# Edge counting of a GPS layer: one-hot tiles made eight at once, two moves on GpSimd's queue, edge slots in two halves

## The reference, cut to what matters

```
xn = layernorm(x)
# graph convolution: 20,625 edges (src, dst), sorted by dst, loops included
deg  = segment_sum(1, dst);  norm = deg[src]^-1/2 * deg[dst]^-1/2
gnn  = segment_sum((xn @ W)[src] * norm, dst) + b
# attention, 12 heads, 266 features
k1 = ratio * (exp(k' - diag_k - max over ALL of k') + 1e-4)     # one maximum for the whole of k'
q1 = ratio * (exp(q' - diag_q - max over features) + 1e-4)
mix = (q1 @ (k1^T v)) / (q1 @ sum k1) @ W_proj + b_proj
x1 = x + gnn + mix
out = x1 + experts(layernorm(x1))      # shared expert plus three of 15 routed ones
```

## Time and profile before

| what | value |
|---|---|
| median of three runs | 1266.8 us (1265.02 to 1268.58) |
| the profiled execution's own time | 1266.61 us |
| its span, first to last instruction | 1264.9 us |
| PE busy, PE weight load | 1146.0 us (91%), 1006.5 us (80%) |
| DVE, ACT, POOL busy | 788.2, 660.2, 499.5 us |
| mean granted TensorE clock | 0.961 |

### The profile page before, as it was taken

The page is one execution under the profiler, slowest core; times in us unless marked ns, Lnnn a source line. Parts: engine busy times, 40 slices in busy tenths (PEclk is TensorE's granted clock), DMA queues, the critical chain, the costliest instruction groups (busy, mean ns, idle before and its releaser), DMA issues.

```text
span 1264.9 us, 20941 instructions
## 1 busy us (share of the span) xinstructions
PE 1146.0 (91%) x6438; PEld 1006.5 (80%) x6439; DVE 788.2 (62%) x1478; ACT 660.2 (52%) x1042; POOL 499.5 (39%) x351
## 2 busy tenths in 40 slices
PE   2999946999549899999999999999999999999985
PEld 1999946887435557888889998888999888899974
DVE  7832613256399584662586597465596698655983
ACT  4122617236210303443687668566677796676863
POOL 1078877888630050026232243121343272323421
PEclk9899977999879899999999999999999999999998
DMA  9030000550110012212678666647657887386943
GB/s 311 1 84 2 2 2 2 138 172 6 15 75 2 1 58 92 88 25 55 219 263 321 225 210 241 201 149 280 214 205 282 306 321 229 134 307 215 347 164 96
DMA packets 62948, 191.72 MB, mean 152 GB/s; under 512 B 14172, under 2 KB 15239, under 8 KB 62902
## 3 DMA queue, kind: packets, MB, share of 16 engines
q1 hardware_dynamic: 50134, 172.52, 37.2%
q0 software_dynamic: 11728, 18.27, 8.2%
q10 hardware_dynamic: 1040, 0.33, 0.1%
HBM read 178.74 MB, written 15.09 MB: 153 GB/s over the span
## 4 chain that ended last, share of the span: by engine, by line
PE 58%; POOL 17%; DVE 10%; issue 7%; DMA 3%; ACT 2%; ACTq 0%; SPq 0%; DVEq 0%; POOLq 0%
PE banks L1910 23%; PE banks L1894 22%; POOL edge_dram L721 17%; PE banks L1832 3%; DVE ohd L966 3%; PE banks L1878 2%; DVE ohs L965 2%; PE banks L1882 2%; PE banks L1804 2%; DMA out<-ysb,sidx 2%; PE banks L1871 1%; PE banks L1652 1%; DVE w2lo L525 1%; DMA xs<-in_x 1%; DMA xn_dram<-xn 1%
## 5 line engine op out<-in xcount | busy, mean ns | idle before, releaser
L721 POOL DMA_INDIRECT edge_dram<-epair,eslot x165 | 216.1, 1310 | 111.1 <-DVE eslot L936 61.4
L800 POOL DMA_INDIRECT out<-ysb,sidx x27 | 118.8, 4399 | 237.1 <-issue 205.8
L512 ACT ACTIVATE w2hi<-w2raw 128x1536 fp32r<-128x1536 f32 x96 | 139.2, 1483 | 90.4 <-DMA w2raw<-in_L_ffn_fc_w 78.9
L525 DVE TENSOR_TENSOR w2lo<-w2raw,w2hi 128x1536 fp32r<-128x1536 f32 x96 | 164.3, 1752 | 22.9 <-ACT w2hi L512 20.7
L1910 PE MATMUL banks<-w2hi,hthi 128*128 128x384 f32 x624 | 161.4, 339 | 0.0
L1910 PE MATMUL banks<-w2lo,hthi 128*128 128x384 f32 x624 | 159.1, 335 | 0.0
L1910 PE MATMUL banks<-w2hi,htlo 128*128 128x384 f32 x624 | 158.9, 335 | 0.0
L512 ACT ACTIVATE w1hi<-w1raw 128x1536 fp32r<-128x1536 f32 x96 | 137.2, 1495 | 27.3 <-DMA w1raw<-in_L_ffn_fc_w 24.7
L525 DVE TENSOR_TENSOR w1lo<-w1raw,w1hi 128x1536 fp32r<-128x1536 f32 x80 | 147.7, 1910 | 0.2 <-DVE xs L1128 0.2
L1894 PE MATMUL banks<-w1hi,xthi 128*128 128x512 f32 x486 | 139.7, 396 | 3.0 <-POOL w1lo L525 3.0
L1894 PE MATMUL banks<-w1lo,xthi 128*128 128x512 f32 x486 | 136.8, 390 | 0.0
(11 more groups left out here) (338 smaller groups left out, 1956.3 us busy)
## 6 DMA issues: line engine op xcount, KB each, us to landing
w1raw<-in_L_ffn_fc_w SPq DMA_DIRECT2D x96, 768.0 KB, 6.6
w2raw<-in_L_ffn_fc_w SPq DMA_DIRECT2D x96, 768.0 KB, 6.1
xs<-in_x SPq DMA_DIRECT2D x10, 336.0 KB
edge_dram<-epair,eslot POOLq DMA_INDIRECT x165, 2.6
wg<-in_L_gnn_W SPq DMA_DIRECT2D x1, 2304.0 KB, 13.7
wv<-in_L_mix_W_qkv SPq DMA_DIRECT2D x1, 2304.0 KB, 20.1
wk<-in_L_mix_W_qkv SPq DMA_DIRECT2D x1, 2304.0 KB, 24.2
wq<-in_L_mix_W_qkv SPq DMA_DIRECT2D x1, 2304.0 KB, 10.8
```

Source lines behind the costliest of these rows:

```text
L512: act.activation(unit(w2hi if second else w1hi, second, u), unit(w2raw if second else w1raw, second, u), ACT.Copy).then_inc(w2_hi if secon ...
L525: eng.tensor_tensor(unit(w2lo if second else w1lo, second, u), unit(w2raw if second else w1raw, second, u), unit(w2hi if second else w1hi, ...
L721: pool.indirect_dma_start(out=edge_dram, out_offset=bass.IndirectOffsetOnAxis(ap=eslot[:, k:k + 1], axis=0), in_=epair[:, k, :].bitcast(I3 ...
L800: pool.indirect_dma_start(out=out, out_offset=bass.IndirectOffsetOnAxis(ap=sidx[:, 0:1], axis=0), in_=ysb[:, :], in_offset=None, bounds_ch ...
```

## The change

The edges are read as 128 partitions by 162 columns (the last column has 17 edges, loaded by two more small DMAs behind a wait for a memset; other rows of it hold -1000 and are not scattered). The slots are worked out in two halves of 81 columns, with `eslot_ok` raised after each. The maximum over partitions goes from column 76 to column 62; the ones for `v` go to VectorE. The keys' bias is worked out ahead of `split_low("q", 1)` and `square("q", 0)`. ScalarE's exponentials of the keys are mixed with the copies of q in halves. Two of the five tiles of `xn` are normalised on VectorE. The output projection's parts 0 to 2 run without counting, parts 3 to 7 with 37 tiles each. The one-hots of eight tiles, source and destination, are made by one tensor-tensor comparison of 128 by 2000 elements in which the tile is the innermost index, so that the two operands of each counting matmul have a stride of 16 elements; the ring holds five such batches.

```
-ET = EDGES // TP
+ET = (EDGES + 127) // 128
+REST = EDGES - 128 * (ET - 1)
-RING = 48
+BATCH, RING = 8, 5
+BATCHES = (ET_TILES + BATCH - 1) // BATCH
-ONES_AT, MAX_AT = 16, 76
+MAX_AT = 62
+HALVES_OF_EDGES = [(0, ET // 2), (ET // 2, ET)]
-TILES_BESIDE = 7 * C
+FIRST_BESIDE, LAST_BESIDE = 3, 8
+def tiles_before(n):
+
+    return ET_TILES * max(0, min(n, LAST_BESIDE) - FIRST_BESIDE) // (LAST_BESIDE - FIRST_BESIDE)
...
+        oh = at("oh", 0, [128, RING, TP, 2 * BATCH], BF16)
+        iota_r = at("iota_r", 20000, [128, TP, 2 * BATCH], F16)
+        ecode = at("ecode", 35008, [128, BATCHES * BATCH, 2], F16)
...
-            groups([("pj", n // 2, n % 2)], [0 if n == 2 * NT - 2 else 7])
-            if n == 2 * NT - 3:
+            groups([("pj", n // 2, n % 2)], [6 if n == 1 else 0 if n == 2 * NT - 1 else 7])
+            if n == 2 * NT - 2:
                 groups([("deg", 0)], [1])
...
+            for n, of in enumerate((src, dst)):
+                sp.dma_start(src_i[:, n, 0:ET - 1], of[0:128 * (ET - 1)].rearrange("(p k) -> p k", p=128)).then_inc(ld_idx, 16)
+            sp.wait_ge(edge_pad, 1)
+            for n, of in enumerate((src, dst)):
+                sp.dma_start(src_i[0:REST, n, ET - 1:ET], of[128 * (ET - 1):EDGES].rearrange("(p k) -> p k", p=REST)).then_inc(ld_idx, 16)
...
-            pool.wait_ge(eslot_ok, 1)
             pool.wait_ge(st_epad, 16)
             for k in range(ET):
-                if k == ONES_AT:
-                    done(pool, ("h", NT - 1, 1))
-                    pool.memset(vext[:, :, :, HD:HD + 1], 1.0).then_inc(vones_ok, 1)
+                for n, (a, b) in enumerate(HALVES_OF_EDGES):
+                    if k == a:
+                        pool.wait_ge(eslot_ok, n + 1)
                 if k == MAX_AT:
                     pool.wait_ge(kmax_ok, 1)
                     pool.partition_all_reduce(kmax[0:TP, 1:2], kmax[0:TP, 0:1], TP, RMAX).then_inc(kall_ok, 1)
...
+            def slots_of(a, b):
+
+                for n in range(BUCKETS):
+                    last = dve.scalar_tensor_tensor(out=epos[:, n, a:b], in0=erun[:, n, a:b], scalar=efrom[:, n:n + 1], in1=ehot[:, n, a:b],
                                                     op0=ALU.add, op1=ALU.mult)
...
-            def one_hots(a, b):
-
-                for t in range(a, b):
-                    if t >= RING:
-                        dve.wait_ge(oh_free, t - RING + 1)
-                    dve.tensor_scalar(ohs[:, t % RING, 0:TP], iota_n[:, :], etab[:, t, 0:1], None, ALU.is_equal)
-                    dve.tensor_scalar(ohd[:, t % RING, 0:TP], iota_n[:, :], etab[:, t, 1:2], None, ALU.is_equal).then_inc(oh_ready, 1)
+            def one_hots(n):
+
+                if n >= RING:
+                    dve.wait_ge(oh_free, n - RING + 1)
+                codes = ecode[:, BATCH * n:BATCH * n + BATCH, :].rearrange("p t c -> p (t c)")
+                dve.tensor_tensor(oh[:, n % RING, :, :], iota_r[:, :, :], codes.unsqueeze(1).broadcast_to([128, TP, 2 * BATCH]),
+                                  ALU.is_equal).then_inc(oh_ready, 1)
...
+            dve.wait_ge(norm_ok, 1)
+            for i in (1, 3):
+                dve.tensor_scalar(xn[:, i, :], xs[:, i, :], lnrs[:, 3, i:i + 1], lnrs[:, 4, i:i + 1], ALU.mult, ALU.add).then_inc(xn_dve, 1)
             dve.wait_ge(const_ok, 1)
-            link(run(0, BUCKETS // 2))
-            for n, (kind, k) in enumerate(T8):
+            link(run(0, 8))
+            for kind, k in T8[:C]:
                 x_lower(kind, k)
             split_low(dve, "h", 0)
-            link(run(BUCKETS // 2, BUCKETS))
+            for kind, k in T8[C:]:
+                x_lower(kind, k)
+            link(run(8, BUCKETS))
             bucket_totals()
             split_low(dve, "h", 1)
             edge_slots()
+            slots_of(*HALVES_OF_EDGES[0])
             split_low(dve, "v", 0)
+            slots_of(*HALVES_OF_EDGES[1])
             tile_regions()
...
-            split_low(dve, "q", 1)
-            square("q", 0)
             squares_to(("sqk", 0), 0)
             dve.wait_ge(kall_ok, 1)
             taken(dve, ("sqk", 0))
             dve.tensor_scalar(nbias[:, 2, :], nbias[:, 0, :], -1.0, kmax[0:TP, 1:2], ALU.mult, ALU.subtract).then_inc(kbias_ok, 1)
+            square("q", 0)
+            split_low(dve, "q", 1)
...
+            dve.tensor_copy(iota_r[:, :, :], iota_n[:, :].unsqueeze(2).broadcast_to([128, TP, 2 * BATCH])).then_inc(iota_r_ok, 1)
+            dve.memset(ecode[:, ET_TILES:, :], -1.0)
...
+            for n in range(FIRST_BESIDE):
+                add_projection(n // 2, n % 2)
+            dve.wait_ge(ld_edges, 16)
+            dve.tensor_copy(ecode[:, 0:ET_TILES, :], etab[:, :, :]).then_inc(iota_r_ok, 1)
+            dve.wait_ge(iota_r_ok, 2)
+            made = 0
+            for n in range(FIRST_BESIDE, LAST_BESIDE):
+                upto = min(BATCHES, RING + tiles_before(n + 1) // BATCH)
+                for batch in range(made, upto):
+                    one_hots(batch)
+                made = upto
+                if n < LAST_BESIDE - 1:
                     add_projection(n // 2, n % 2)
...
-            add_projection(3, 0)
-            add_projection(3, 1)
+            for n in range(LAST_BESIDE - 1, 2 * NT - 1):
+                add_projection(n // 2, n % 2)
...
-            rows_times("h", {2: bucket_ranks})
+            rows_times("h", {1: bucket_ranks})
...
+            def counts_begin():
+
+                pe.wait_ge(ld_offs, 16)
+                pe.wait_ge(eye_ok, 2)
+                taken(pe, ("pj", 0, 1))
...
-                    pe.wait_ge(oh_ready, t + 1)
-                    last = pe.matmul(banks[0:TP, bass.ds(where[t % OFFSETS], TP)], ohs[:, t % RING, 0:TP], ohd[:, t % RING, 0:TP],
+                    pe.wait_ge(oh_ready, t // BATCH + 1)
+                    made, k = oh[:, t // BATCH % RING, :, :], 2 * (t % BATCH)
+                    last = pe.matmul(banks[0:TP, bass.ds(where[t % OFFSETS], TP)], made[:, :, k], made[:, :, k + 1],
                                      start=False, stop=t == ET_TILES - 1, skip_group_check=True)
-                    last.then_inc(oh_free, 1)
+                    if t % BATCH == BATCH - 1:
+                        last.then_inc(oh_free, 1)
...
+                if n == FIRST_BESIDE:
+                    counts_begin()
...
-            for n in range(2 * NT - 2):
+            for n in range(2 * NT - 1):
                 project_out(n)
...
-            project_out(2 * NT - 2)
             project_out(2 * NT - 1)
-            pe.wait_ge(h_scaled, NT)
...
+                        pe.wait_ge(h_scaled, b + 1)
```

More of the change, by code:

```diff
@@ L450, in taken, with turn_tokens @@
             eng.wait_ge(free[b], n)
-        def turn_tokens(pe, name, rows, ready, per_tile, after=lambda n: None):
-            for n, (kind, k) in enumerate(T8):
+        def turn_tokens(pe, name, rows, ready):
+            for kind, k in T8:
                 ps = fill(pe, (name, kind, k))
@@ L919, in edge_slots @@
-                for b in range(BUCKETS):
-                    last = dve.scalar_tensor_tensor(out=epos[:, b, :], in0=erun[:, b, :], scalar=efrom[0:TP, b:b + 1], in1=ehot[:, b, :],
+                link(dve.tensor_tensor(efrom[:, 1:BUCKETS], efrom[:, 1:BUCKETS], elast[:, 0:BUCKETS - 1], ALU.subtract))
+            def slots_of(a, b):
+                for n in range(BUCKETS):
+                    last = dve.scalar_tensor_tensor(out=epos[:, n, a:b], in0=erun[:, n, a:b], scalar=efrom[:, n:n + 1], in1=ehot[:, n, a:b],
@@ L1010, in _ @@
             split_low(dve, "k", 1)
+            done(dve, ("h", NT - 1, 1))
+            dve.memset(vext[:, :, :, HD:HD + 1], 1.0).then_inc(vones_ok, 1)
             def square(name, o):
@@ L1358, in _ @@
             act.wait_ge(norm_ok, 1)
-            for i in range(NT):
+            for i in (0, 2, 4):
                 act.wait_ge(ld_x[i], 32)
@@ L1385, in take_rows, with take_columns @@
                 emptied(ins, (name, i, s))
-            def take_columns(name, o):
-                for s, (a, b) in enumerate(TSPLIT):
+            def take_columns(name, o, parts=(0, 1)):
+                for s in parts:
+                    a, b = TSPLIT[s]
                     ps = read(act, (name, o, s))
@@ L1410, in copy_keys, with exp_keys @@
                     emptied(act.activation(kfeat[:, i, h, :], ps[0:TP, 0:M], ACT.Copy), ("ddk", i, h))
-            def exp_keys(i):
+            def exp_keys(i, part=None):
                 act.wait_ge(kbias_ok, 1)
-                for h in range(H):
+                for h in range(H) if part is None else range(6 * part, 6 * part + 6):
                     n = H * i + h
                     last = act.activation(kfeat[:, i, h, :], kfeat[:, i, h, :], ACT.Exp, bias=nbias[:, 2, n:n + 1])
-                last.then_inc(kexp_ok, 1)
+                if part != 0:
+                    last.then_inc(kexp_ok, 1)
             act.wait_ge(st_bias, 32)
@@ L1618, in _ @@
             filled(last, ("lt", 0))
```

(23 more changed lines are left out.)

140 lines of the change are left out of this document (65 added, 75 removed).

## The result

The changed kernel took 1401.3 us (median of 4 executions, 1398.16 to 1405.46) against 1266.99 (1265.02 to 1268.58) of the kernel before on the same chip: ratio 1.106, interval 1.103 to 1.110. It was forecast at 1233 and came out 134 us slower than before. Its span was 1400.4 us, the mean granted clock of TensorE 0.916 instead of 0.961.

The account below looks back on a forecast made before the run. POOL's scatter stream, then DVE's one-hots and a tail, was taken to bound the messages' start. Counting done 32.4 us earlier plus 1.6 in the tail gave 34.0: span 1230.9, median 1233, range 1214 to 1249.

Parts of the forecast that it names:

- part 2: POOL's scatter stream: end 12.5 us earlier, with a 128-row scatter assumed to cost the same as a 125-row one.
- part 3: Maximum over partitions and attention: keys' bias 30.7 us earlier, attention hidden behind the scatters with 13 us of slack.
- rival of cheap scatters: POOL's 128-row scatters take 1.02 instead of 1.19 us, 27.7 us off the stream, time 1217; chance 0.12.
- Step 1: POOL's first scatter: 10.8 us earlier, at 55.4 us instead of 66.18.
- Step 2: POOL's scatter stream: 270.7 us long, ending at 326.1; 3 us of it for the second half of `epos`.
- Step 3: Maximum ends at 164.3, attention at 303; TensorE idle from about 321, with 8.1 us for transposes and two parts.
- Step 4, last scatter to the converted codes: After POOL's last scatter: bias sums, DVE's additions, first projection parts and the codes' conversion, done after 15.3 us.
- Step 4, codes to counted: Counting parts on DVE and TensorE: 10.5 + 28.5 + 8.1 us, batches 1.11, strided tiles 0.10; counted at 388.5.
- My factor of 1.79: TensorE's counting tile: DVE's strided against contiguous price per element, taken to raise 0.0575 us to 0.10.
- the 0.28 from which I had said that the change turns to a loss: Deciding tile time of the slower rival, strided operands on TensorE at 0.48 us a tile, 1303 us; chance 0.06.
- the 0.19 that my range took in: TensorE's stride cost in us a tile up to which the range 1214 to 1249 was meant to hold.
- Step 5: Tail from counted to messages, 23.6 us before: net 1.6 us less, with 2.2 given back at the third messages group.

Follow-up runs that it names:

- e1: Changed kernel with the edges laid out as before, 125 partitions x 165 columns and 125-row scatters; 1272.3 us, ratio 1.004.
- e2: Kernel before with only the 128-partition layout and 128-row scatters; 1232.6 us, ratio 0.973.
- e16: Same kernel as e2, run again in a later session; 1380.8 us.
- e3: Changed kernel with at most 2 scatters under way instead of 8, still 128 rows each; 1270.1 us.
- e15: Same kernel as e3, run again in a later session; 1396.4 us.
- e9: e1 with 4 operands innermost in the one-hot tiles, a stride of 8 bytes instead of 32; 1247.7 us, ratio 0.987.
- e10: e1 with the one-hot part undone, one-hots made tile by tile as in the kernel before; 1253.9 us, ratio 0.991.
- e18: e9 with the sum of biases and its addition to xs on DVE behind attention instead of on POOL; 1233.95 us, ratio 0.974.
- e11: Changed kernel on 128 partitions with only rows 0 to 111 sent per scatter, an eighth of the edges left out; 1219.9 us.
- e4: Changed kernel on 128 partitions with only rows 0 to 124 sent per scatter, 2.3% of the edges left out; 1294.5 us.
- e13: e1 with 126 partitions x 164 columns and 126-row scatters instead of 125; 1395.7 us.

## Why the prediction was wrong, step by step

**The step that failed** is the assumption at the end of part 2, "what a scatter of 128 rows costs beside 125: I take the same", and with it part 3, which rested on a TensorE that runs through. On POOL such a scatter costs less (0.97 for 1.19 us); on TensorE it can cost 2.5 us of standing in front of each matmul. Of the 168 us between 1233 and 1401, 129 lie between e1 (1272.3) and the changed kernel: the stall, less what the shorter scatters give back. By itself the stall is dearer in two of three comparisons: 148 us between e2 and e16 and 126 between e3 and e15, the same kernels, and by estimate 157 to 160 in the changed kernel (1401.3 less the 1241 to 1244 below). My rival of cheap scatters had POOL's side right, from the gathers of 128 rows, at 1.02 us a scatter. None of my cases had a scatter that goes with idle time of an engine that waits for no data and no semaphore of it. Nothing in the trace of before could have shown it, but "no row shows it" should have been a reason for a wide upper bound, not for "the same".

The other 39 us are seen in e1 without the stall, in these terms. The trace of e1 is of an execution 2.6 us above its median.

- *Step 1, first scatter 55.4:* 54.96, in e1 55.38. Right.
- *Step 2, end of the stream 326.1:* in e1 330.5. That layout has three columns more, 3 x 1.49 = 4.5 us. Right, for the period that I took, but one term by luck: the 3 us for the second half of `epos` are there because a single scatter, at 58.38, took 4.91 us. In e9, e10 and e18 the same scatter took 1.33 or 1.34 and those behind it 1.21 to 1.23, so `epos` costs some 0.2 us, and the stream of e9 ends at 328.1.
- *Step 3, maximum and attention:* with TensorE fed, right. The maximum came at 164.87 (forecast end 164.3). Attention ended at 306.7 (forecast 303), and TensorE idled from 320.6 us on (forecast 321). The text of the forecast does not add up, 303 and 8.1 are 311: transposes and two parts took 13.9.
- *Step 4, last scatter to the converted codes, 15.3 us:* 23.0, from 330.53 to 353.48. I let POOL's bias addition start right behind the memset of `bsplit`. The earlier trace rows had it otherwise, 340.69 + 2.02 and then nothing before the sum of biases at about 350. In e1, POOL's timeline:

```profile
332.60 2.02 POOL L743 MEMSET bsplit<- 128x2304 bf16 x1
341.75 1.79 POOL L746 TENSOR_TENSOR bias<-bias 125x768 f32<-125x768 f32 x1 [7.14 <-issue]
343.62 8.86 POOL L750 TENSOR_TENSOR xs<-xs,bias 125x768 f32<-125x768 f32 x5
```

  7.1 us of "issue" that were there to be read. e18 moves them off the path, behind a POOL that nobody waits for.
- *Step 4, codes to counted, 47.1 us:* 73.9, to 427.4. The batch was right: 1.20 us against 1.19, at the 16-bit rate. The tile was not: I took 0.10 us for it and measured 0.227. The steps of e1, six tiles and two projection matmuls in 2.03 us:

```profile
392.15 0.83 PE L1849 MATMUL banks<-wp,aot 128*125 128x384 f32 x2
392.82 1.54 PE L1833 MATMUL banks<-oh 128*125 128x125 bf16 x6
394.18 0.83 PE L1849 MATMUL banks<-wp,aot 128*125 128x384 f32 x2
394.84 1.54 PE L1833 MATMUL banks<-oh 128*125 128x125 bf16 x6
```

  From 392.82 to 394.18 are 1.36 us for six. With 4 operands innermost, in e9, the same eight matmuls take 1.33 to 1.35 us, and six tiles 0.67:

```profile
373.09 0.83 PE L1853 MATMUL banks<-wp,aot 128*125 128x384 f32 x2
373.76 0.84 PE L1837 MATMUL banks<-oh 128*125 128x125 bf16 x6
374.42 0.84 PE L1853 MATMUL banks<-wp,aot 128*125 128x384 f32 x2
375.10 0.85 PE L1837 MATMUL banks<-oh 128*125 128x125 bf16 x6
```

  185 tiles by 0.115 us are 21 us; the counting, from the first tile on, became 25.8 shorter (354.85 to 427.4 against 352.36 to 399.2), the time 24.6. Most of the rest is the clock. While e1 counted, with no gap over 1.3 us on TensorE, the granted clock fell to 0.50 again and again (372 to 376, 384 to 388 and 416 to 420 us); in e9 it stayed at 1.00. At 0.50 two projection matmuls take 1.25 us instead of 0.67, but the six tiles 1.39 instead of 1.36:

```profile
371.93 1.57 PE L1833 MATMUL banks<-oh 128*125 128x125 bf16 x6
373.32 1.46 PE L1849 MATMUL banks<-wp,aot 128*125 128x384 f32 x2
374.57 1.56 PE L1833 MATMUL banks<-oh 128*125 128x125 bf16 x6
```

  13 pairs slowed so, in whole or in part, are about 7 us. With 23.5 us by estimate for 185 tiles at 0.127 over my price that is more than the 26.8 missed; what part of it other waits hid I did not follow. My factor of 1.79 was that of DVE's strided reading, another engine's; the true one is 4. It stayed under the 0.28 from which I had said that the change turns to a loss, but over the 0.19 that my range took in. With the 7 us of POOL it was enough: with 125 rows the new one-hots cost 18.4 us against the old (e1 less e10, across two sessions) and gain 6.2 with the shorter stride (e10 less e9, in one).
- *Step 5, the tail:* from counted to messages 21.0 us, forecast 22, with the 2.2 us given back later already in it. From messages to the end 824.7 us instead of 820.4, so 4.3 more. DVE's splits of w1 stand in front of the first norm; in e9 and e18, where the messages start earlier still, it is 827 to 828.

The terms add up: 4.4 + 7.7 + 26.8 - 1.0 are 37.9, and messages start in e1 at 448.46 for 410.5 forecast; with the 4.3 behind them that is its span of 1273.2 for 1230.9. Without the stall the changed kernel would, by an estimate from e11's messages (414.39) and the 825 to 828 us behind them, have taken 1241 to 1244 us: against my forecast the earlier stream takes back most of the dear tiles. No run of it escaped the stall, and that time, inside my range, would have been the right number by luck.

**What stays open.** What in a session makes the stall is not known, nor whether the state that shows as missing landing times and "remote" waits is its cause. It was seen with scatters of 126 and of 128 rows, never with 125; 112 rows were run in one session only, one without the stall, and the layout of 128 partitions with 125 rows sent (e4) too, so whether the rows or the layout keep a kernel safe is not shown apart. In the changed kernel it begins 38 and 61 us after a run of scatters begins, some 30 and 48 scatters, and it ends with a pause of POOL. Which resource TensorE shares with them, and whether it is its supply of instructions, was not shown. Nor is it explained that POOL, behind `bsplit`, stands about 17 us in the stalled kernels (16.94 in the changed kernel) and about 7 in the others.

## What to carry to other kernels

A time from one session is one draw: repeat a kernel that is far off beside its parent in another session before you explain it by its edits; here the same code gave 1232.6 and 1380.8 us. Such a session may be told from the trace of a kernel that does not stall: in e18 the scatters had no landing time. When an engine is idle on "issue" while nothing it waits for is late, look at what the DMA queues are doing at that moment, and keep a long stream of indirect DMAs in a form that was seen to be harmless (here 125 rows) even where another is 0.2 us cheaper each. A row's start, length and next start must be read together: the 7 us of idle that I stepped over stood between two rows that I quoted.

## What the runs showed of the hardware

- A scatter's price did not follow the number of its rows: 112 rows 0.94 us (e11), 125 rows 1.19 (e1), 126 rows 0.98 (e13), 128 rows 0.97 (the changed kernel).
- In the stall TensorE starts instructions at distances of about 0.70 us and its multiples (2.80 us between the matmuls above; 0.70, 0.71, 0.70 and 1.39 between 351.52 and 355.02), at a granted clock of 0.50, the lower level of 1.2 GHz. After its end at 146 us the clock was back (0.77 over 140 to 160 us, 1.00 from 160).
- TensorE reading two bf16 operands: 0.0575 us a tile of 128 by 125 when both are contiguous, 0.112 when both have a stride of 8 bytes (e9), 0.227 at 32 (e1), and 0.23 at 32 also when the granted clock was halved: a strided tile hardly follows the clock. The Trainium skill (SBUF — State Buffer, Specifications) asks for two hits in a line of 16 bytes for full bandwidth. At 8 bytes there are two, and the tile still took twice the contiguous time; the measurement decides.
